# A two-layer attention and MLP kernel: second MLP product from fp16 halves, and small steps moved between VectorE, ScalarE and GpSimd

## The chip, the cores and the metric

The kernel runs as one program on one NeuronCore of a Trainium2 chip. The metric is device time in microseconds (us), from the start of the program to its end, as the median of several executions. One execution was also recorded by the hardware profiler; its rows are quoted below. Five engines work in parallel, each through its own queue in program order: TensorE (PE in the profile; PEld is its weight load), VectorE (DVE), ScalarE (ACT), GpSimd (POOL) and SyncE (SP), which here issues all DMAs. They meet only at semaphores.

## The reference, cut to what matters

The input x is 4 x 2048 x 256 in float32. Two blocks follow one another, each wrapped in layer normalisations and a residual sum:

```
x = x + layernorm(A(layernorm(x)))      # A: full self-attention over each batch of 2048 rows, softmax over axis 1
x = x + layernorm(F(layernorm(x)))      # F: two layers as below
layer(x):
    h = shift_token(x); q, k, v = split(h @ wqkv)         # 8 heads of 64
    q = l2norm(q) * q_scale; k = l2norm(k) * k_scale; q, k = rotary_xpos(q, k)
    o = local_attention(q, k, v)                          # windows of 128 rows, own window and the one before
    x = x + o @ wo
    h = layernorm(shift_token(x)) * ln_g + ln_b
    a, g = split(h @ w1 + b1)                             # 2 x 682 columns
    x = x + (a * gelu(g)) @ w2 + b2                       # w2: 682 x 256, "the second MLP product"
```

## The kernel before, in words

`phase_a` computes A batch by batch and writes the normalised result, the stream of layer one, to DRAM. `phase_b` computes F. It has a prologue, a block of its own in which weights are loaded, scaled and split, and then the main block.

Splitting is how float32 products are made here. A value is split into a high part, rounded to a narrower type, and a low part, the value less its high part; three products (high x high, high x low, low x high: `PARTS`) stand for the full one. In the main block wqkv, wo and the scores go through the fp32r type in this way, and w1 with its input h2T through fp16. The exception is the second MLP product (L955): it multiplies `hid` by `w2`, both plain float32, in 12 products of 128x256 for two windows; the profile has 24 records for them, two for each product.

The main block treats a stream of 128 windows of 128 rows (64 for each layer). All five engines run the same sequence of slots, written out by hand in a function `run(s, r, pairs, layer)`; four slots are unrolled in a loop (`slots`). In slot s TensorE does, in this order: transposes of qr and kr of window s-1 (L847, L854), the q, k and v projections of window s (L869), transposes of the probabilities of window s-2 (L885) and their product with v (L897), scores of window s-1 (L910), the wo product of window s-2 (L923), transposes of the next window's input (L836). The MLP works on pairs of windows: an even slot ends with the first MLP product (L944, 66 records), the odd slot after it with the second (L955). So a pair of slots is one period. The order inside each engine's `run` is fixed, and a wait at any place holds back all that is behind it on that engine.

The other engines in a slot, as far as the change touches them:

- ScalarE: copies of qT and kT, squares of q and k (`sq`, L981 and L983), copy of v (L986), four copies of transposed probabilities (`probsT`, L992), copy of oT (L995), eight exponentials (L1002), in even slots six gelus (L1015).
- VectorE: low parts of qT and kT (L1098, L1100), in even slots the pair's output sum `layer_output` (L1063), statistics of the MLP input h2 (L1107, L1109, L1111), the rotary products of q in three pieces (L1041 to L1043), the normalised MLP input `xh` and its fp16 high part (L1117, L1120), the rotary products of k, in odd slots of layer two the statistics of the final normalisation (`output_stats`), low part of oT (L1090), eight masked score passes (L1138) with `floor_norms` (L1050) inside them, then reciprocals and normalisations of the probabilities in pairs (L1148, L1151), with the residual sum xp (L1162) behind the second pair, in odd slots of layer two `output_norm` (L1084), in even slots six products with the gelu (`hid`, L1174).
- GpSimd: the power that gives 1/std of the MLP input (L1200), six halvings that sum the 64 squares of each head (`halve`, L1190), the low part of xh (L1205), qr (L1209) and the sum of k's rotary terms (L1212), in odd slots of layer two a power for the final normalisation (L1218), the power that gives the 16 inverse norms `rn` (L1223), kr = terms x inverse norms (L1228), the sum xb (L1234), in odd slots of layer two the final residual sum (L1240). kr of window s is what TensorE transposes at L854 near the start of slot s+1.
- SyncE: xp goes to DRAM and comes back, shifted by one row, as h2 (L819, L823, L824); the two fp16 halves of xh are transposed by a DMA into h2T (L813).

## Time and profile before

| | us |
|---|---|
| median of 3 executions | 3123.78 (3122.63 to 3124.51) |
| the profiled execution, its time | 3122.74 |
| its span, first to last instruction | 3120.9 |

The busy shares of the span are PE 95%, PEld 83%, DVE 85%, ACT 60% and POOL 56%. `phase_a` fills the first 650 us, the prologue lasts to about 717 us, and the main block has the rest. A row of the profile's groups gives line, engine, operation, output<-input, count, busy time and mean duration; a row of a timeline gives start, duration and the same names, with the idle time ahead of it in brackets where there was some.

### The profile page before, as it was taken

The page shows a single profiled execution, that of the slowest core. Times are in us where ns is not written, and L with a number is a line of the kernel's source. Part 1 is how long each engine was busy: PE and PEld are TensorE (multiplying, and loading weights), DVE is VectorE, ACT ScalarE, POOL GpSimd, SP SyncE. Part 2 cuts the span into 40 slices and gives each one's busy share as a digit, 9 for nine tenths or more (in the row PEclk, how much of TensorE's full clock was granted, in tenths as well). Part 3 has the DMA queues.
Part 4 walks back from the last instruction along what each step waited for, and adds up shares of the span by engine and source line. Part 5 has one row for each costly group of instructions (what it writes and reads, how often), then busy time and mean ns, then how long its engine had stood idle before and what let it go on. Part 6 is the DMA issues. An engine that isn't in the chain of part 4 may idle for free.

```text
span 3120.9 us, 79791 instructions
## 1 busy us (share of the span) xinstructions
PE 2969.0 (95%) x24952; PEld 2577.5 (83%) x24952; DVE 2654.2 (85%) x7701; ACT 1876.3 (60%) x4322; POOL 1742.8 (56%) x2070
## 2 busy tenths in 40 slices
PE   7999999945999999999999999999999999999997
PEld 4868686844888888888888888888888888888886
DVE  7889898656888888888888888898999999999995
ACT  6252525113666666667666766666666667666763
POOL 0313131125666666666666666676776677767763
PEclk9999999967999999999999999999999999999998
DMA  1212121151111111111111111122221211122121
GB/s 39 62 48 64 46 63 40 54 202 53 47 50 49 56 47 50 52 49 47 50 54 50 49 54 48 51 57 61 61 56 58 59 55 55 58 64 59 56 58 43
DMA packets 273326, 177.65 MB, mean 57 GB/s; under 512 B 95758, under 2 KB 271090, under 8 KB 272754
## 3 DMA queue, kind: packets, MB, share of 16 engines
q1 hardware_dynamic: 273138, 175.50, 19.2%
q8 instruction: 74, 1.21, 0.2%
q14 instruction: 114, 0.93, 0.1%
HBM read 104.08 MB, written 54.54 MB: 51 GB/s over the span
## 4 chain that ended last, share of the span: by engine, by line
PE 73%; POOL 1%; issue 1%; DVE 1%; ACT 0%; DMA 0%; POOLq 0%; SPq 0%; DVEq 0%; ACTq 0%
PE b_ps L869 17%; PE b_ps L944 14%; PE b_ps L955 10%; PE b_ps L897 8%; PE b_ps L885 7%; PE b_ps L923 6%; PE b_ps L910 6%; PE b_ps L854 2%; PE b_ps L847 2%; PE b_ps L836 1%; POOL b_sq L1190 0%; POOL b_rn L1223 0%; DVE b_probs L1138 0%; POOL b_t L1212 0%; DVE b_probs L1151 0%
## 5 line engine op out<-in xcount | busy, mean ns | idle before, releaser
L1002 ACT ACTIVATE b_probs<-b_probs,b_negmax 128x256 f32<-128x256 f32 x1024 | 505.9, 495 | 78.4 <-DVE b_negmax L1138 77.5
L869 PE MATMUL b_ps<-b_wqkv,b_hT_hi 128*128 128x512 f32 x1536 | 492.0, 402 | 1.0 <-DVE b_hT_lo L1026 1.0
L944 PE MATMUL b_ps<-b_h2T,b_w 128*128 128x256 f16 x4224 | 474.4, 274 | 6.4 <-DMA b_h2T<-b_xh_hl 6.4
L944 PEld LDWEIGHTS b_ps<-b_h2T,b_w 128*128 128x128 f16 x4224 | 414.5, 98 | 55.3 <-DMA b_h2T<-b_xh_hl 6.8
L1190 POOL TENSOR_TENSOR b_sq<-b_sq 128x512 f32<-128x512 f32 (+5 forms) x768 | 418.5, 545 | 60.6 <-ACT b_sq L983 20.3
L1223 POOL TENSOR_TENSOR b_rn<-b_ss_min,b_mhalf 128x16 f32<-128x16 f32 x128 | 377.5, 2949 | 109.2 <-DVE b_ss_min L1050 109.0
L1151 DVE TENSOR_SCALAR b_probs<-b_probs,b_rinv 128x256 f32<-128x256 f32 x1024 | 409.6, 442 | 18.2
L1200 POOL TENSOR_TENSOR b_rstd<-b_var,b_mhalf 128x1 f32<-128x1 f32 x128 | 72.0, 562 | 552.9 <-DVE b_var L1111 552.9
L452 PE MATMUL a_ps<-a_xn_hl,a_E 128*128 128x256 f16 x3072 | 344.5, 273 | 8.8 <-DVE a_E L318 8.8
L955 PE MATMUL b_ps<-b_w,b_hid 128*128 128x256 f32 x1536 | 342.2, 379 | 1.2 <-DVE b_hid L1174 1.2
L452 PEld LDWEIGHTS a_ps<-a_xn_hl,a_E 128*128 128x128 f16 x3072 | 299.4, 98 | 44.2 <-ACT a_e L397 9.6
L869 PEld LDWEIGHTS b_ps<-b_wqkv,b_hT_hi 128*128 128x128 f32 x1536 | 282.7, 191 | 54.3 <-ACT b_hT_hi L967 1.4
L1138 DVE CUSTOM_DVE_ANT_0 b_probs<-b_ps,b_mask,b_rn 128x256 f32<-128x256 f32 x768 | 324.5, 478 | 0.0
L955 PEld LDWEIGHTS b_ps<-b_w,b_hid 128*128 128x128 f32 x1536 | 286.8, 190 | 37.9 <-DVE b_hid L1174 1.5
L869 PE MATMUL b_ps<-b_wqkv,b_hT_lo 128*128 128x512 f32 x768 | 302.7, 394 | 0.0
L992 ACT COPY b_probsT<-b_ps 128x512 f32<-128x512 f32 x512 | 264.0, 611 | 4.5 <-PE b_ps L885 4.2
L1015 ACT ACTIVATE b_gl<-b_ps,b_b,b_w_unit 128x256 f32<-128x256 f32 (+1 forms) x384 | 202.8, 561 | 102.8 <-DVE b_hid L1174 70.4
L897 PE MATMUL b_ps<-b_probsT,b_v 128*64 128x128 f32 x4096 | 252.3, 276 | 0.0
L885 PE MATMUL b_ps<-b_ident_f,b_probs 128*128 128x128 f32 x2048 | 245.5, 273 | 3.5 <-DVE b_xpp L1063 2.3
L885 PEld LDWEIGHTS b_ps<-b_ident_f,b_probs 128*128 128x128 f32 x2048 | 232.2, 141 | 20.0 <-DVE b_xpp L1063 2.5
L897 PEld LDWEIGHTS b_ps<-b_probsT,b_v 128*64 128x64 f32 x4096 | 221.4, 137 | 21.6 <-ACT b_probsT L992 18.1
L1174 DVE SCALAR_TENSOR_TENSOR b_hid<-b_ps,b_b1a,b_gl 128x256 f32<-128x256 f32 (+1 forms) x384 | 177.0, 478 | 53.3 <-ACT b_gl L1015 46.9
(139 smaller groups left out, 6218.8 us busy)
## 6 DMA issues: line engine op xcount, KB each, us to landing
b_hx<-xs_dram SPq DMA_DIRECT2D x256, 64.0 KB, 1.9
b_rot<-rot_dram SPq DMA_DIRECT2D x128, 128.0 KB, 2.1
b_xr<-xs_dram SPq DMA_DIRECT2D x128, 128.0 KB, 2.0
xp_dram<-b_xp SPq DMA_DIRECT2D x128, 128.0 KB, 1.8
b_h<-xp_dram SPq DMA_DIRECT2D x256, 64.0 KB, 1.8
a_x_res<-in_L_attn_x_dram SPq DMA_DIRECT2D x64, 128.0 KB, 2.2
x_dram<-a_x SPq DMA_DIRECT2D x64, 128.0 KB, 1.7
xs_dram<-a_xo SPq DMA_DIRECT2D x64, 128.0 KB, 1.8
```

Of the source, the lines that this page charges most:

```text
L452: last = nc.tensor.matmul(ps[:, bank, 0:D], E[:, j, a, i * P:(i + 1) * P], xn_hl[:, b % 2, j, c, :], start=(j == 0 and a == 0 and c == 0), ...
L869: last = nc.tensor.matmul(ps[:, bank, :], hT[:, k, :], wqkv[:, ds(layer(s), 1), part, k, bank * INNER:(bank + 1) * INNER], start=(k == 0 a ...
L885: last = nc.tensor.transpose(ps[:, 3 + p, n * P:(n + 1) * P], probs[:, 2 * p + n // 2, (n % 2) * P:(n % 2 + 1) * P], ident_f[:])
L897: last = nc.tensor.matmul(ps[h * DH:(h + 1) * DH, 7, p * P:(p + 1) * P], v[:, window, (2 * p + h) * DH:(2 * p + h + 1) * DH], probsT[:, p, ...
L944: last = nc.tensor.matmul(ps[:, bank, half * 2 * P:(half + 1) * 2 * P], w1[:, ds(layer(2 * j), 1), wp, k, first:first + P], h2T[:, hp, k, ...
L955: last = nc.tensor.matmul(ps[:, 3, n * D:(n + 1) * D], hid[:, c, n * P:(n + 1) * P], w2[:, ds(layer(2 * j), 1), c, :], start=(c == 0), sto ...
L992: nc.scalar.copy(probsT[:, p, :], ps[:, 3 + p, :]).then_inc(pT_kept, 1)
L1002: nc.scalar.activation(probs[:, h, :], probs[:, h, :], ACT.Exp, bias=negmax[:, h:h + 1], scale=-1.0, accum_out=rowsum[:, h:h + 1]).then_in ...
L1138: nc.vector.tensor_tensor_reduce(probs[:, h, :], head_scores(h), which, rn[:, (r - 1) % 2, h:h + 1], ABOVE_ALL, ALU.add, ALU.min, negmax[: ...
L1151: nc.vector.tensor_scalar(probs[:, h, :], probs[:, h, :], rinv[:, h:h + 1], None, ALU.mult).then_inc(probs_ready, 1)
L1190: nc.gpsimd.tensor_tensor(target, target, sq[:, :, width:2 * width], ALU.add).then_inc(ss_halved, 1)
L1223: nc.gpsimd.tensor_tensor(rn[:, r % 2, :], ss_min[:], mhalf[:], ALU.pow).then_inc(rn_ready, 1)
```

## The change

- The second MLP product: w2 is kept as two fp16 halves, scaled by a power of two, and the pair's output sum multiplies by `w2_unit` to undo the scale (one operation with a product and a sum in place of a plain sum). `hid` is split into two fp16 halves by GpSimd (`hid_halves`: a copy and a subtraction for each of 6 blocks; four blocks at the end of GpSimd's even slot, two early in the odd one). TensorE then does 36 fp16 products of 128x256 in place of the 12 float32 ones, and waits for `hid_lo` in place of `hid_ready`.
- The prologue: w2 and b1 are loaded ahead of the rotary table and wqkv; bounds for the scale of `hid` are found by further reductions on VectorE and a second all-reduce on GpSimd; w1 is scaled in two column parts, each split in its own instruction; w2 is scaled and split; three of the five masks are copied in SBUF instead of loaded.
- The MLP input: `xh` and its fp16 high part are made by ScalarE (`normalise_input`, two activations with scale and bias), in even slots ahead of the probability copies, in odd slots behind them and behind v's copy. The epsilon sum and the bias are made by GpSimd (`var2`, `shift2`). VectorE keeps the statistics, now ahead of `layer_output`.
- The final normalisation: `varf` and `shiftf` on GpSimd, the normalisation itself on ScalarE.
- The sums of squares: one halving on GpSimd, the rest as one reduction on VectorE (`sum_squares`), the floor on GpSimd; the power of 16 columns becomes one of 8 for k, ahead of kr, and one of 8 for q, behind it ("powers behind their sum").
- VectorE: the rotary products of a tensor in two instructions (the second reads the halves in reversed order) in place of three; reciprocals for four heads at a time in place of two.

The main block's part of the diff (semaphore declarations and changed counts left out):

```diff
-                        pe.wait_ge(hid_ready, HC * (j + 1))
+                        pe.wait_ge(hid_lo, HC * (j + 1))
                         if in_range(s - 1):
                             pe.wait_ge(scores_kept, HEADS * (s - 1) + BANK_READ[3])
                         for n in range(2):
                             for c in range(HC):
-                                last = nc.tensor.matmul(ps[:, 3, n * D:(n + 1) * D], hid[:, c, n * P:(n + 1) * P], w2[:, ds(layer(2 * j), 1), c, :],
-                                                        start=(c == 0), stop=(c == HC - 1))
+                                for a, (hp, wp) in enumerate(PARTS):
+                                    last = nc.tensor.matmul(ps[:, 3, n * D:(n + 1) * D], hid_hl[:, hp, c, n * P:(n + 1) * P],
+                                                            w2[:, ds(layer(2 * j), 1), wp, c, :],
+                                                            start=(c == 0 and a == 0), stop=(c == HC - 1 and a == 2))
...
+                def normalise_input(t, r):
+                    if in_range(t):
+                        act.wait_ge(shift2_ready, t + 1)
+                        wait(act, xh_lo, t)
+                        nc.scalar.activation(xh[:], h2[:, (r - 3) % 2, :], ACT.Identity, bias=shift2[:], scale=rstd2[:]).then_inc(xh_ready, 1)
+                        wait(act, h2T_loaded, 16 * t)
+                        nc.scalar.activation(xh_hl[:, 0, :], h2[:, (r - 3) % 2, :], ACT.Identity, bias=shift2[:], scale=rstd2[:]).then_inc(xh_hi, 1)
...
-                        wait(act, ss_ready, s)
+                        wait(act, ss_summed, s)
                         act.wait_ge(q_done, s + 1)
                         nc.scalar.activation(sq[:, 0:HEADS, :], by_head(ps[:, 0, :]), ACT.Square).then_inc(q_sq, 1)
                         act.wait_ge(k_done, s + 1)
                         nc.scalar.activation(sq[:, HEADS:2 * HEADS, :], by_head(ps[:, 1, :]), ACT.Square).then_inc(k_sq, 1)
-                        act.wait_ge(v_done, s + 1)
-                        wait(act, pv_done, s - 2)
-                        nc.scalar.copy(v[:, r, :], ps[:, 2, :]).then_inc(v_kept, 1)
+                    if r % 2 == 0:
+                        normalise_input(s - 3, r)
                     t = s - 2
                     if in_range(t):
                         wait(act, pv_done, t)
                         for p in range(HP):
                             act.wait_ge(pT_done, HP * t + p + 1)
                             nc.scalar.copy(probsT[:, p, :], ps[:, 3 + p, :]).then_inc(pT_kept, 1)
+                    if in_range(s):
+                        act.wait_ge(v_done, s + 1)
+                        wait(act, pv_done, s - 2)
+                        nc.scalar.copy(v[:, r, :], ps[:, 2, :]).then_inc(v_kept, 1)
+                    if r % 2 == 1:
+                        normalise_input(s - 3, r)
...
+                        act.wait_ge(shiftf_ready, f + 1)
+                        wait(act, fin_stored, 16 * f)
+                        for n in range(2):
+                            nc.scalar.activation(fin[:, n, :], xpp[:, n, :], ACT.Identity, bias=shiftf[:, n:n + 1], scale=rstdf[:, n:n + 1]).then_inc(xf_ready, 1)
...
+                        nc.vector.tensor_tensor(by_head(t1[:, n, :]), by_head(ps[:, n, :]), factor(2 * n), ALU.mult).then_inc(terms, 1)
+                                                factor(2 * n + 1).rearrange("p h (c d) -> p h c d", c=2), ALU.mult).then_inc(terms, 1)
...
+                def norm_stats(s, r):
+                    t = s - 3
+                    if in_range(t):
+                        dve.wait_ge(h2_loaded, 32 * (t + 1))
+                        nc.vector.bn_stats(st2[:], h2[:, (r - 3) % 2, :]).then_inc(st2_ready, 1)
+                        wait(dve, shift2_ready, t)
+                        wait_apart(dve, st2_ready, t + 1, passed_dve)
+                        nc.vector.bn_aggr(mv2[:], st2[:]).then_inc(mv2_ready, 1)
...
+                            nc.vector.scalar_tensor_tensor(xpp[:, n, :], ps[:, 3, n * D:(n + 1) * D], w2_unit[:, ds(layer(2 * j), 1)], xb[:, (r - 6 + n) % 4, :],
+                                                           ALU.mult, ALU.add).then_inc(xpp_ready, 1)
...
                     layer_output(pairs - 3, r, layer)
-                    t = s - 3
-                    if in_range(t):
-                        dve.wait_ge(h2_loaded, 32 * (t + 1))
-                        nc.vector.bn_stats(st2[:], h2[:, (r - 3) % 2, :]).then_inc(st2_ready, 1)
-                        wait_apart(dve, st2_ready, t + 1, passed_dve)
-                        nc.vector.bn_aggr(mv2[:], st2[:]).then_inc(mv2_ready, 1)
-                        dve.wait_ge(mv2_ready, t + 1)
-                        nc.vector.tensor_scalar(var2[:], mv2[:, 1:2], EPS, None, ALU.add).then_inc(var2_ready, 1)
                     rotate(s, r, 0, q_sq, q_terms, qr_ready)
-                    t = s - 3
-                    if in_range(t):
-                        dve.wait_ge(rstd2_ready, t + 1)
-                        wait(dve, xh_lo, t)
-                        nc.vector.tensor_scalar(xh[:], h2[:, (r - 3) % 2, :], mv2[:, 0:1], rstd2[:], ALU.subtract, ALU.mult).then_inc(xh_ready, 1)
-                        dve.wait_ge(xh_ready, t + 1)
-                        wait(dve, h2T_loaded, 16 * t)
-                        nc.vector.tensor_copy(xh_hl[:, 0, :], xh[:]).then_inc(xh_hi, 1)
                     rotate(s, r, 1, k_sq, k_terms, kr_ready)
                     output_stats(pairs - 3, r, layer)
+                    sum_squares(s)
                     oT_low(s - 2)
...
+                            if p % 2 == 0:
+                                dve.wait_ge(exp_done, HEADS * t + 2 * p + 4)
+                                nc.vector.reciprocal(rinv[:, 2 * p:2 * p + 4], rowsum[:, 2 * p:2 * p + 4]).then_inc(rinv_ready, 1)
+                                dve.wait_ge(rinv_ready, 2 * t + p // 2 + 1)
...
-                def halve(s, first, end):
-                    if in_range(s):
-                        pool.wait_ge(k_sq, s + 1)
-                        for n in range(first, end):
-                            width = DH >> (n + 1)
-                            target = sq[:, :, 0:width]
-                            wait(pool, ss_halved, HALVINGS * s + n)
-                            nc.gpsimd.tensor_tensor(target, target, sq[:, :, width:2 * width], ALU.add).then_inc(ss_halved, 1)
+                def hid_halves(j, first, end):
+                    if in_range(2 * j):
+                        wait(pool, w2_done, j)
+                        for c in range(first, end):
+                            rows = slice(0, P if c < FULL else REST)
+                            wait_apart(pool, hid_ready, HC * j + c + 1, passed_pool)
+                            nc.gpsimd.tensor_copy(hid_hl[rows, 0, c, :], hid[rows, c, :]).then_inc(hid_hi, 1)
+                            pool.wait_ge(hid_hi, HC * j + c + 1)
+                            nc.gpsimd.tensor_tensor(hid_hl[rows, 1, c, :], hid[rows, c, :], hid_hl[rows, 0, c, :], ALU.subtract).then_inc(hid_lo, 1)
                 def run(s, r, pairs, layer):
                     if r == 0 and in_range(s):
                         nc.gpsimd.tensor_copy(mask_now[:], mask[:, ds((s // SLOTS) % (WPB // SLOTS), 1), :]).then_inc(mask_ready, 1)
                     t = s - 3
                     if in_range(t):
+                        wait_apart(pool, mv2_ready, t + 1, passed_pool)
+                        nc.gpsimd.tensor_scalar(var2[:], mv2[:, 1:2], EPS, None, ALU.add).then_inc(var2_ready, 1)
                         pool.wait_ge(var2_ready, t + 1)
+                        wait(pool, xh_hi, t)
                         nc.gpsimd.tensor_tensor(rstd2[:], var2[:], mhalf[:, 0:1], ALU.pow).then_inc(rstd2_ready, 1)
-                    halve(s, 0, 2)
-                    if in_range(t):
+                        wait_apart(pool, rstd2_ready, t + 1, passed_pool)
+                        nc.gpsimd.tensor_scalar(shift2[:], mv2[:, 0:1], rstd2[:], -1.0, ALU.mult, ALU.mult).then_inc(shift2_ready, 1)
+                    if in_range(s):
+                        pool.wait_ge(k_sq, s + 1)
+                        nc.gpsimd.tensor_tensor(sq[:, :, 0:DH // 2], sq[:, :, 0:DH // 2], sq[:, :, DH // 2:DH], ALU.add).then_inc(ss_halved, 1)
+                    if r % 2 == 1:
+                        hid_halves(pairs - 2, HID_EARLY, HC)
+                    t = s - 3
+                    if in_range(t):
+                        pool.wait_ge(xh_ready, t + 1)
                         pool.wait_ge(xh_hi, t + 1)
                         wait(pool, h2T_loaded, 16 * t)
                         nc.gpsimd.tensor_tensor(xh_hl[:, 1, :], xh[:], xh_hl[:, 0, :], ALU.subtract).then_inc(xh_lo, 1)
                     if in_range(s):
-                        pool.wait_ge(q_terms, 3 * (s + 1))
+                        pool.wait_ge(q_terms, 2 * (s + 1))
                         wait(pool, qT_done, s)
                         nc.gpsimd.tensor_tensor(qr[:], t1[:, 0, :], t2[:, 0, :], ALU.add).then_inc(qr_ready, 1)
-                        halve(s, 2, HALVINGS)
-                        pool.wait_ge(k_terms, 3 * (s + 1))
+                        pool.wait_ge(k_terms, 2 * (s + 1))
                         nc.gpsimd.tensor_tensor(t1[:, 1, :], t1[:, 1, :], t2[:, 1, :], ALU.add).then_inc(kr_sum, 1)
                     j = pairs - 3
                     f = j - NW // 2
                     if r % 2 == 1 and in_range(2 * j) and layer(2 * j) == 1:
+                        wait_apart(pool, mvf_ready, 2 * f + 2, passed_pool)
+                        nc.gpsimd.tensor_scalar(varf[:], mvf[:, :, 1], EPS, None, ALU.add).then_inc(varf_ready, 1)
                         pool.wait_ge(varf_ready, f + 1)
+                        wait(pool, xf_ready, 2 * f)
                         nc.gpsimd.tensor_tensor(rstdf[:], varf[:], mhalf[:, 0:2], ALU.pow).then_inc(rstdf_ready, 1)
+                        wait_apart(pool, rstdf_ready, f + 1, passed_pool)
+                        for n in range(2):
+                            last = nc.gpsimd.tensor_scalar(shiftf[:, n:n + 1], mvf[:, n, 0:1], rstdf[:, n:n + 1], -1.0, ALU.mult, ALU.mult)
+                        last.then_inc(shiftf_ready, 1)
                     if in_range(s):
+                        wait_apart(pool, ss_summed, s + 1, passed_pool)
+                        nc.gpsimd.tensor_scalar(ss_min[:], ss[:], 1e-24, None, ALU.max).then_inc(ss_ready, 1)
                         pool.wait_ge(ss_ready, s + 1)
-                        wait(pool, scores_kept, HEADS * (s - 1))
-                        nc.gpsimd.tensor_tensor(rn[:, r % 2, :], ss_min[:], mhalf[:], ALU.pow).then_inc(rn_ready, 1)
-                    if in_range(s):
-                        pool.wait_ge(rn_ready, s + 1)
+                        nc.gpsimd.tensor_tensor(rn_k[:], ss_min[:, HEADS:2 * HEADS], mhalf[:, 0:HEADS], ALU.pow).then_inc(rnk_ready, 1)
+                        pool.wait_ge(rnk_ready, s + 1)
                         pool.wait_ge(kr_sum, s + 1)
                         wait(pool, kT_done, s)
                         nc.gpsimd.tensor_tensor(by_head(kr[:]), by_head(t1[:, 1, :]),
-                                                rn[:, r % 2, HEADS:2 * HEADS].unsqueeze(2).to_broadcast([P, HEADS, DH]), ALU.mult).then_inc(kr_ready, 1)
+                                                rn_k[:].unsqueeze(2).to_broadcast([P, HEADS, DH]), ALU.mult).then_inc(kr_ready, 1)
+                        wait(pool, scores_kept, HEADS * (s - 1))
+                        nc.gpsimd.tensor_tensor(rn[:, r % 2, :], ss_min[:, 0:HEADS], mhalf[:, 0:HEADS], ALU.pow).then_inc(rn_ready, 1)
                     t = s - 2
                     if in_range(t):
                         pool.wait_ge(xp_ready, t + 1)
                         wait(pool, xpp_ready, t - 3)
                         nc.gpsimd.tensor_tensor(xb[:, (r - 2) % 4, :], xp[:, r % 2, :], b2[:, ds(layer(t), 1), :], ALU.add).then_inc(xb_ready, 1)
+                    if r % 2 == 0:
+                        hid_halves(pairs - 2, 0, HID_EARLY)
```

## Rows read from the trace of the kernel before

**Rows 1.** The page: busy time, share of the span and instructions of each engine.

```profile
PE 2969.0 (95%) x24952; PEld 2577.5 (83%) x24952; DVE 2654.2 (85%) x7701; ACT 1876.3 (60%) x4322; POOL 1742.8 (56%) x2070
```

**Rows 2.** Stretches: busy us of each engine, granted clock, DMA share, GB/s.

```profile
1496.90:1533.50 36.60, 36.60 (x317) 32.68 (x315) 31.64 (x99) 25.19 (x63) 23.67 (x27) 1.00 0.17 50
2630.90:2667.60 36.70, 36.70 (x317) 32.59 (x315) 33.66 (x106) 25.02 (x63) 25.97 (x29) 1.00 0.20 57
```

**Rows 3.** Timeline of PE over one pair of slots.

```profile
1496.75 7.37 PE L944 MATMUL b_ps<-b_h2T,b_w 128*128 128x256 f16 x66
1503.95 0.60 PE L847 MATMUL b_ps<-b_ident_f,b_qr 128*128 128x128 f32 x4
...
1510.80 1.97 PE L897 MATMUL b_ps<-b_probsT,b_v 128*64 128x128 f32 x32
...
1516.05 5.34 PE L955 MATMUL b_ps<-b_w,b_hid 128*128 128x256 f32 x24
1521.23 0.60 PE L847 MATMUL b_ps<-b_ident_f,b_qr 128*128 128x128 f32 x4
1521.67 0.60 PE L854 MATMUL b_ps<-b_ident_f,b_kr 128*128 128x128 f32 x4
```

**Rows 4.** Timeline of POOL, the same pair: kr of the odd slot.

```profile
1519.81 1.04 POOL L1228 TENSOR_TENSOR b_kr<-b_t,b_rn 128x512 f32<-128x512 f32 x1
```

**Rows 5.** Groups of instructions on POOL, by line.

```profile
L1223 POOL TENSOR_TENSOR b_rn<-b_ss_min,b_mhalf 128x16 f32<-128x16 f32 x128 | 377.5, 2949 | 109.2 <-DVE b_ss_min L1050 109.0
...
L1212 POOL TENSOR_TENSOR b_t<-b_t 128x512 f32<-128x512 f32 x128 | 165.5, 1293 | 0.0
...
L1205 POOL TENSOR_TENSOR b_xh_hl<-b_xh,b_xh_hl 128x256 f16<-128x256 f32 x128 | 86.4, 675 | 40.0 <-DVE b_xh_hl L1120 40.0
...
L1200 POOL TENSOR_TENSOR b_rstd<-b_var,b_mhalf 128x1 f32<-128x1 f32 x128 | 72.0, 562 | 552.9 <-DVE b_var L1111 552.9
...
L1218 POOL TENSOR_TENSOR b_rstdf<-b_varf,b_mhalf 128x2 f32<-128x2 f32 x32 | 22.6, 707 | 19.3 <-DVE b_varf L1075 15.8 <-DMA b_x<-x_dram 3.5
...
L1196 POOL COPY b_mask_now<-b_mask 128x256 bf16 (+1 forms) x32 | 13.8, 430 | 0.0
...
L223 POOL TENSOR_TENSOR a_rstd_c<-a_pow_c,a_unscale 128x1 f32<-128x1 f32 x64 | 12.1, 189 | 5.0
...
L210 POOL TENSOR_TENSOR a_rstd_first<-a_var_first,a_mhalf 128x4 f32<-128x4 f32 x4 | 4.8, 1198 | 13.8 <-DVE a_var_first L276 13.8
```

**Rows 6.** Timeline of DVE, ACT and SP in the same pair.

```profile
1504.74 1.06 DVE L1174 SCALAR_TENSOR_TENSOR b_hid<-b_ps,b_b1a,b_gl 128x256 f32<-128x256 f32 x2 [0.26 <-ACT b_gl L1015]
...
1507.71 0.18 DVE L1109 BATCH_NORM_AGGREGATE b_mv<-b_st 128x2 f32<-128x6 f32 x1 [0.15 <-DVE b_st L1107]
...
1502.95 1.02 ACT L1015 ACTIVATE b_gl<-b_ps,b_b,b_w_unit 128x256 f32<-128x256 f32 x2 [1.06 <-DVE b_hid L1174]
...
1507.79 0.60 ACT L983 ACTIVATE b_sq<-b_ps 128x512 f32<-128x512 f32 x1 [0.72 <-PE b_ps L869]
...
1509.64 2.06 ACT L992 COPY b_probsT<-b_ps 128x512 f32<-128x512 f32 x4
1512.81 0.59 ACT L995 CAST b_oT<-b_ps 128x512 fp32r<-128x512 f32 x1 [1.11 <-PE b_ps L897]
...
1521.65 0.38 SPq L824 DMA_DIRECT2D b_h<-xp_dram  x1
```

**Rows 7.** Groups on DVE in the prologue, and its last instruction there (timeline).

```profile
L654 DVE TENSOR_REDUCE p_top<-p_w_f 128x1 f32<-128x2816 f32 x2 | 6.2, 3086 | 0.1
...
715.85 0.36 DVE L681 TENSOR_SCALAR b_b1a<-b_b,p_w_scale 128x6 f32<-128x6 f32 x2
```

**Rows 8.** The page's DMA issues: output<-input, count, size, us from issue to landing.

```profile
b_h<-xp_dram SPq DMA_DIRECT2D x256, 64.0 KB, 1.8
```

**Rows 9.** The chain that ended last, first slots of the main block.

```profile
726.91 1.30 POOL b_sq L1190
...
736.01 1.05 POOL b_kr L1228
```

200 lines of the change are left out of this document (115 added, 85 removed).

## The prediction

> **What bounds the kernel now.** I read first the busy shares and the busy time by stretch. PE is busy 95% of the span [rows 1], and in a period of the main block it is busy all of it: 36.6 of 36.6 us in layer one and 36.7 of 36.7 in layer two, at a granted clock of 1.00 (2.4 GHz), with DVE at 31.6 and 33.7 and POOL at 23.7 and 26.0 [rows 2]. So the period is TensorE's own work, and only less of that work, or a new wait of PE, moves it. Second, PE's timeline, for the length of the slots. I count from the start of the odd slot, 1503.95, as 0: the second MLP product stands at 12.10 to 17.28, then come the next slot's q transposes, and its k transposes at 17.72 [rows 3]. Third, POOL's timeline, for the one result that comes near its need: kr for that even slot is done at 1520.85, which is 16.90, 0.8 ahead of its use [rows 3, 4]. Last the groups by line, for prices.
>
> **The product.** The float32 form takes 5.18 us a pair (1516.05 to 1521.23). The fp16 form is the shape of the first MLP product, which runs 66 records in 7.20 us, 0.109 each [rows 3]; 36 of them are 3.93 us. Gain 1.25 us a pair. Of the 64 pairs two fall in the drain, so 62 x 1.25 = 77.5 us, if nothing new is late. The odd slot becomes 16.03 long, and kr is needed at 16.47.
>
> **GpSimd's odd slot, layer one.** Prices on POOL: a power of 1, 2, 4 and 16 columns took 0.56, 0.71, 1.20 and 2.95 us [rows 5]. One of 8 columns lies between 1.20 and 2.95; on the line through those two it is 1.78, which I take. The small steps (`var2`, `shift2`, floor, `varf`, `shiftf`) have as nearest row a 1-column product at 0.19; their ends are 0.10 and the 0.56 of the power; I take 0.19, plus 0.1 where a wait stands ahead. A float32 to fp16 copy of 256 columns has the mask's copy, 0.43, as nearest row; its ends are 0.2 and the 0.675 of the two-input subtraction into fp16; I take 0.43. The subtraction itself is that 0.675 row [rows 5]. The two-input passes of 512 columns are 1.29 (the first halving 1.30) [rows 5, 9].
> The order is then: mv2 from DVE at 3.94 (DVE's place for it is unmoved) [rows 6]; `var2`, power, `shift2` 1.21, so 5.15; k's squares are done by 4.44 [rows 6], so the halving ends at 6.45; blocks 4 and 5 of `hid`, which DVE ends by about 1.85 [rows 6], cost 1.27 each (copy, subtraction, 0.17 of waits): 9.0. The high part of xh comes from ACT: probability copies from about 5.5 to 7.5, v 0.5, two activations that I price as the pair of gelus, 1.02 [rows 6]: 9.0 as well. Low part 0.75: 9.75. qr and k's sum 2.5: 12.25. Floor 0.3, power 1.85, kr 1.1: 15.5. That is 1.0 ahead of 16.47, about the room there was. The four blocks of the even slot's end don't reach in: the first block of `hid` is there at about -1.15, four cost 5.0 at most, 3.9 is just ahead of mv2. Layer one keeps its full gain: of the 62 steady pairs 33 run before the final normalisation's steps begin, 33 x 1.25 = 41.
>
> **Layer two.** Here the odd slot also holds `varf`, its power, and two `shiftf`: 0.29 + 0.78 + 0.48 = 1.55, ahead of kr. So kr comes at 17.05, 0.6 late, where before `varf` was DVE's and the powers stood in room. Behind it wait q's power 1.78, xb 0.7 to 0.8 and the final sum 1.29; GpSimd is then at about 20.9, 4.9 into the even slot, plus 0.46 for the mask in every other one. `var2` to `shift2` takes 1.21 more, and now ACT stands at `normalise_input` ahead of the probability copies: shift2 at 6.1 or 6.55, activations to 7.1 or 7.6, first copy 0.5 later, 7.6 or 8.1. PE wants it for its product with v at 6.85 [rows 3] plus the 0.6 that it is already late: another 0.15 or 0.65, on average 0.4. Together 1.0 lost of 1.25, so 29 x 0.25 = 7 gained.
> The Trainium skill (GPSIMD Engine Reference, Engine selection) advises against GpSimd for elementwise work, two-input operations being about twice VectorE's time and one-input ones roughly line rate. The rows agree on the first (675 and 1293 ns for 256 and 512 columns); by the second a copy would be an estimated 0.1 shorter than mine, kr 0.2 earlier, and the sum 6 lower.
>
> **What is taken from other engines** costs nothing in a period, since PE hides it. DVE loses xh and its cast, the third rotary piece, half of the reciprocals, and gains one reduction of 512 columns, about 0.6 by 1.1 ns a column [rows 7], between k's rotation and oT's low part, where it waited anyhow. The h2 load ends 1.8 after its issue at 1521.65 [rows 6, 8], 19.5, which in a shorter odd slot is 3.5 into the even one: mv2 comes 0.8 later there than before, at about 4.2, shift2 at 5.4, ACT's activations end at 6.4 and the first copy at 6.9, against 6.85. That costs 0.05 at most in layer one; without the move ahead of `layer_output` it would cost 0.7. In the odd slot ACT ends its activations at 9.0 and took oT up at 8.86 before [rows 6]: 0.15 late, and the wo product has about as much room. I take zero for it, with 0.2 a slot as the other end.
>
> **The start of the main block.** The first four slots are a chain through GpSimd: from k's squares at 726.9 to kr at 737.1, 10.2 us [rows 9]. New: halving 1.3, qr and sum 2.55, floor 0.3, power 1.85, kr 1.1: 7.1. That is 3 us in each of four slots, 12; between 6 (where PE and the scores take over as the bound) and 15.
>
> **The prologue** ends with DVE, at 716.2 [rows 7]. DVE must now finish w2's maxima before the scale is known (3072 columns at 1.1 ns, 3.4 [rows 7]), run some 12 more small steps (2), and split w2 (3.3): 9 in all. The ends are 2 (the shorter mask copy, less contention) and 20 (wqkv lands behind 1.4 MB more). The sum takes 9.
>
> **The drain.** The last two blocks of `hid` are halved behind the last gelu, 1.7 to 2 us; the final normalisation's small steps add 0.6 twice; the product is 1.25 shorter: +2, between -1 and +6.
>
> **Sum,** against the profiled execution's own 3122.7 (the span is 1.8 less, and the median of the runs 1.0 more, which I leave): 3122.7 + 9 - 12 - 41 - 7 + 2 = 3074.
>
> **Rivals.**
> - GpSimd keeps up in layer two as well: its small steps overlap, or copies are at their lower end. For it: kr is only 0.6 late by my count, within the error of seven estimated steps. Against it: POOL would be busy over 90% of a layer-two period. 3122.7 + 9 - 12 - 77.5 + 2 = 3044.
> - ScalarE's new order delays oT in the odd slot or the copies in the even one, by 0.2 each, in all pairs: 62 x 0.4 = 25 less gain, 3098. For it: 0.0 to 0.15 of room. Against: DVE is earlier now.
> - The other side: GpSimd's chain from mv2 to kr is late in layer one and far too late in layer two. With every unknown half way to its upper end (copy 0.55, power 2.37, small steps 0.375) the chain is 1.4 longer in layer one: kr 0.45 late, gain 33 x 0.8 = 26. In layer two it is 2.0 longer, kr at 19.0, 2.55 late, and with rn, xb and the final sum behind it the even slot's first copy 1.0 late: 3.55 - 1.25 = 2.3 lost in 29 pairs, 67. 3122.7 - 1 - 26 + 67 = 3163, slower. It decides from about 1.7 us more a pair than I have counted for layer two.
> - ACT needs another table for Identity: a load of 1.28 ahead of each use, 2.6 a pair in ACT's two tight places, 62 x 1.35 = 84 more, 3206. The trace before has copies and squares beside Exp and Gelu without loads of their own, no row has Identity. The Trainium skill (ScalarE: Activation LUTs, Table sets: the hidden batching unit) names identity among the fillers in every set, which speaks against this.
> - The change doesn't do what it says: three fp16 products take as long as the float32 one, by weight loads. Against it, the 66 records beside it [rows 3]. 3122, within 0.2%.
>
> **Chances.** Forecast 0.45 (its own range 3055 to 3095); full gain 0.30; ScalarE's order 0.10; GpSimd late in both 0.08; tables 0.03; no shorter product 0.04. A measurement of this kernel tells 0.2%, 6 us, from no change. Faster 0.86 (the first three, and a little), same 0.05, slower 0.09. The range leaves out the slow cases and the edge of the full gain: 3035 to 3115.
>
> **What would show it.** The second product at 3.9 us a pair. A layer-one period of 35.3 with PE without a gap; a layer-two period of about 36.3 with two waits of PE, k transposes on kr (0.6) and the product with v on `probsT` (0.4), and POOL at over 32 us busy. Ramp slots 3 us shorter, prologue 9 longer. It is wrong if layer one shows a wait of PE above 0.3 a pair, if layer two shows none or over 2 us, or if the power of 8 columns is over 2.3 us.

## The result, and the profile after

The changed kernel takes 3157.46 us (median of 4 runs, 3153.39 to 3158.82) against 3123.2 for the kernel before, timed beside it: ratio 1.0108, interval 1.009 to 1.0125. It is slower by 34 us; the forecast was 3074. The profiled execution has a span of 3157.0, 36.1 longer than before.

The page of the changed kernel, busy time by engine, against [rows 1]:

```profile
PE 2926.8 (93%) x25720; PEld 2507.4 (79%) x25720; DVE 2415.2 (77%) x6734; ACT 2036.9 (65%) x4644; POOL 2065.3 (65%) x2807
```

PE is busy 42 us less and the kernel is 36 longer, so PE is idle 78 us more. In PE's groups by line the second product alone fell by 77 us (342.2 to 264.9, L955 and L1007); the rest of PE's busy time rose by 35, 10 of it in the projections and 9 in the product with v. Two stretches, one period of layer one and one of layer two, with the columns of [rows 2]:

```profile
1521.70:1558.10 36.40, 35.99 (x329) 31.53 (x328) 28.37 (x85) 27.09 (x66) 28.18 (x38) 1.00 0.18 51
2672.10:2709.60 37.50, 35.94 (x329) 31.57 (x328) 29.01 (x89) 28.21 (x69) 30.89 (x42) 1.00 0.20 56
```

Before, PE was busy for the whole of either period. Now 0.4 and 1.6 are idle, at the full granted clock. From the starts of the 64 first MLP products the span divides like this (us, against the kernel before):

| stretch | forecast | measured |
|---|---|---|
| up to the first MLP product (802.1 to 805.0) | -3 | +2.9 |
| its pairs 0 to 32, period 36.56 to 36.46 | -41 | -3 |
| pairs 32 to 62, period 36.57 to 37.66 from pair 34 on | -7 | +31 |
| from pair 62's to the end (51.7 to 56.7) | +2 | +5 |

The next table tells where in a slot it stands. It has the mean start of each of TensorE's products, counted from the slot's first q transpose, over 20 pairs of layer one (L1) and 24 of layer two (L2), read from the timelines of PE. I use it for every kernel below. Columns: k transposes (kr), projections (qkv), transposes of probabilities (pT), product with v (pv), wo, MLP product (w1 or w2), end of the slot.

```
kernel    slot     kr    qkv   pT    pv    wo     mlp    end
before    even L1  0.44  0.79  4.99  6.83  10.34  12.09  19.29
before    odd  L1  0.44  0.79  4.99  6.83  10.34  12.08  17.27
changed   even L1  0.44  0.79  5.35  7.47  11.13  12.87  20.08
changed   even L2  2.03  2.44  6.71  8.78  12.44  14.18  21.39
changed   odd  both 0.44 0.79  5.07  6.91  10.62  12.36  16.29
a3        even L1  0.43  0.79  5.07  6.91  10.48  12.40  19.61
a4        even L2  0.61  1.20  5.52  7.56  11.22  12.96  20.16
b1        even L1  0.44  1.46  5.91  8.04  11.70  13.44  20.65
b1        even L2  0.44  1.21  5.53  7.51  11.17  12.91  20.12
d1        even L1  0.44  0.79  5.07  6.91  10.49  12.41  19.62
d1        even L2  0.61  1.20  5.49  7.33  10.91  12.84  20.05
d4        even L1  0.44  1.38  5.68  7.51  11.01  12.75  19.96
d4        odd  L2  0.43  0.79  5.07  6.91  12.44  14.19  18.18
```

The second product did become 1.25 shorter: the odd slot's last part is 3.93 (16.29 - 12.36), as worked out from [rows 3]. The even slot gave it back, 0.8 in layer one and 2.1 in layer two.

**Layer two.** The timeline of PE and POOL in the changed kernel, the end of an odd slot that began at 2655.82:

```profile
2672.11 0.60 PE L898 MATMUL b_ps<-b_ident_f,b_qr 128*128 128x128 f32 x4
2674.14 0.66 PE L905 MATMUL b_ps<-b_ident_f,b_kr 128*128 128x128 f32 x4 [1.43 <-POOL b_kr L1301]
...
2663.48 0.67 POOL L1245 TENSOR_TENSOR b_hid_hl<-b_hid,b_hid_hl 42x256 f16<-42x256 f32 x1
2665.41 0.68 POOL L1272 TENSOR_TENSOR b_xh_hl<-b_xh,b_xh_hl 128x256 f16<-128x256 f32 x1 [1.26 <-ACT b_xh_hl L1029]
2666.05 1.27 POOL L1276 TENSOR_TENSOR b_qr<-b_t 128x512 f32<-128x512 f32 x1
2667.28 1.28 POOL L1278 TENSOR_TENSOR b_t<-b_t 128x512 f32<-128x512 f32 x1
2668.64 0.23 POOL L1284 TENSOR_SCALAR b_varf<-b_mvf 128x2 f32<-128x2 f32 x1
2668.95 0.73 POOL L1287 TENSOR_TENSOR b_rstdf<-b_varf,b_mhalf 128x2 f32<-128x2 f32 x1
2669.90 0.59 POOL L1290 TENSOR_SCALAR b_shiftf<-b_mvf,b_rstdf 128x1 f32<-128x1 f32 x2 [0.22 <-POOL b_rstdf L1287]
2670.57 0.39 POOL L1295 TENSOR_SCALAR b_ss_min<-b_ss 128x16 f32<-128x16 f32 x1
2671.05 1.83 POOL L1297 TENSOR_TENSOR b_rn_k<-b_ss_min,b_mhalf 128x8 f32<-128x8 f32 x1
2672.97 1.04 POOL L1301 TENSOR_TENSOR b_kr<-b_t,b_rn_k 128x512 f32<-128x512 f32 x1
```

Read GpSimd's rows as one queue. It is full from `xh_lo` (L1272) to kr (L1301) and ends 18.2 after the slot's start, where 16.5 was wanted; ahead of `xh_lo` it stands idle for 1.26 and waits for ScalarE. The changed kernel's waits of PE, columns: waiting line, releaser, total us, times, longest:

```profile
PE b_ps L905 <- POOL b_kr L1301: 48.8, 31, 3.8
```

**Layer one.** The even slot that begins at 1558.08, timelines of four engines:

```profile
1561.64 0.43 DVE L1130 BATCH_NORM_STATS2 b_st<-b_h 128x6 f32<-128x256 f32 x1 [0.94 <-DMA b_h<-xp_dram]
1562.20 0.18 DVE L1133 BATCH_NORM_AGGREGATE b_mv<-b_st 128x2 f32<-128x6 f32 x1
1562.51 0.88 DVE L1146 SCALAR_TENSOR_TENSOR b_xpp<-b_ps,b_w_unit,b_xb 128x256 f32<-128x256 f32 x2
...
1563.68 0.27 POOL L1260 TENSOR_SCALAR b_shift<-b_mv,b_rstd 128x1 f32<-128x1 f32 x1 [0.21 <-POOL b_rstd L1258]
...
1563.98 0.60 ACT L1027 ACTIVATE b_xh<-b_h,b_shift,b_rstd 128x256 f32<-128x256 f32 x1 [1.44 <-POOL b_shift L1260]
1564.49 0.59 ACT L1029 ACTIVATE b_xh_hl<-b_h,b_shift,b_rstd 128x256 f16<-128x256 f32 x1
1564.98 2.02 ACT L1053 COPY b_probsT<-b_ps 128x512 f32<-128x512 f32 x4
...
1563.52 1.96 PE L936 MATMUL b_ps<-b_ident_f,b_probs 128*128 128x128 f32 x16 [0.21 <-DVE b_xpp L1146]
1565.60 2.12 PE L948 MATMUL b_ps<-b_probsT,b_v 128*64 128x128 f32 x32
```

Two waits follow from the same DMA. VectorE's output sum stands behind the statistics, which wait 0.94 for h2; the transposes of the probabilities need the PSUM bank that this sum reads, so they start at 5.44. And ScalarE's copies stand behind `xh`, which waits 1.44 for shift2, so the product with v starts at 7.5.

### The profile page after: what moved, and what is told of

It is laid out like the page before. It is cut to its first block and busy times, and to the rows that moved or that the text cites. A ratio compares the mean times of both kernels' runs of the same rounds, so it can differ in the third digit from the quotient of the medians.

```text
span 3157.0 us, 81578 instructions
## 1 busy us (share of the span) xinstructions
PE 2926.8 (93%) x25720; PEld 2507.4 (79%) x25720; DVE 2415.2 (77%) x6734; ACT 2036.9 (65%) x4644; POOL 2065.3 (65%) x2807
## 5 line engine op out<-in xcount | busy, mean ns | idle before, releaser
L920 PE MATMUL b_ps<-b_wqkv,b_hT_hi 128*128 128x512 f32 x1536 | 498.9, 406 | 1.9 <-DVE b_hT_lo L1102 1.0
L1206 DVE TENSOR_SCALAR b_probs<-b_probs,b_rinv 128x256 f32<-128x256 f32 x1024 | 345.7, 389 | 9.0
L1163 DVE TENSOR_TENSOR b_oT<-b_ps,b_oT 128x512 fp32r<-128x512 f32 x128 | 88.5, 692 | 326.0 <-ACT b_oT L1064 326.0
L1194 DVE CUSTOM_DVE_ANT_0 b_probs<-b_ps,b_mask,b_rn 128x256 f32<-128x256 f32 x768 | 317.7, 479 | 0.0
L1245 POOL TENSOR_TENSOR b_hid_hl<-b_hid,b_hid_hl 128x256 f16<-128x256 f32 (+1 forms) x384 | 258.4, 673 | 30.8
L948 PE MATMUL b_ps<-b_probsT,b_v 128*64 128x128 f32 x4096 | 260.8, 280 | 12.0 <-ACT b_probsT L1053 10.2
L1007 PE MATMUL b_ps<-b_w,b_hid_hl 128*128 128x256 f16 x2304 | 264.9, 274 | 3.0 <-POOL b_hid_hl L1245 3.0
L1007 PEld LDWEIGHTS b_ps<-b_w,b_hid_hl 128*128 128x128 f16 x2304 | 226.5, 98 | 30.2 <-POOL b_hid_hl L1245 3.2
L1243 POOL CAST b_hid_hl<-b_hid 128x256 f16<-128x256 f32 (+1 forms) x384 | 152.3, 397 | 123.7 <-DVE b_hid L1228 102.5
L1297 POOL TENSOR_TENSOR b_rn_k<-b_ss_min,b_mhalf 128x8 f32<-128x8 f32 x128 | 219.0, 1711 | 10.7
```

The lines of the kernel that those rows point to most:

```text
L920: last = nc.tensor.matmul(ps[:, bank, :], hT[:, k, :], wqkv[:, ds(layer(s), 1), part, k, bank * INNER:(bank + 1) * INNER], start=(k == 0 a ...
L948: last = nc.tensor.matmul(ps[h * DH:(h + 1) * DH, 7, p * P:(p + 1) * P], v[:, window, (2 * p + h) * DH:(2 * p + h + 1) * DH], probsT[:, p, ...
L1007: last = nc.tensor.matmul(ps[:, 3, n * D:(n + 1) * D], hid_hl[:, hp, c, n * P:(n + 1) * P], w2[:, ds(layer(2 * j), 1), wp, c, :], start=(c ...
L1194: nc.vector.tensor_tensor_reduce(probs[:, h, :], head_scores(h), which, rn[:, (r - 1) % 2, h:h + 1], ABOVE_ALL, ALU.add, ALU.min, negmax[: ...
L1206: nc.vector.tensor_scalar(probs[:, h, :], probs[:, h, :], rinv[:, h:h + 1], None, ALU.mult).then_inc(probs_ready, 1)
L1245: nc.gpsimd.tensor_tensor(hid_hl[rows, 1, c, :], hid[rows, c, :], hid_hl[rows, 0, c, :], ALU.subtract).then_inc(hid_lo, 1)
```

## The experiments

Theory of waits: the new orders hold TensorE in four places (kr in layer two, the output sum, the probability copies, oT), and the product is as good as forecast. The rival put the loss in slower instructions, contention or the clock. Each kernel is timed beside the kernel before. Line numbers are each kernel's own.

**a1, a2, a3: the orders of the even slot.**

```diff
 # a1, VectorE                                 # a2, ScalarE; a3 = a1 + a2
+layer_output(pairs - 3, r, layer)             -if r % 2 == 0: normalise_input(s - 3, r)
 norm_stats(s, r)                               (four copies to probsT)
-layer_output(pairs - 3, r, layer)             +if r % 2 == 0: normalise_input(s - 3, r)
```

> On VectorE layer_output stands ahead of norm_stats again, as before the change; all else is the changed kernel. Theory of waits: in even slots the output sum no longer waits for h2's load, so TensorE's transposes of the probabilities start at about 5.0 us in the even slot in place of 5.4. But ScalarE's probability copies stay behind normalise_input, which waits for shift2, and mv2 now comes 0.7 later; so the product with v does not come earlier and may come up to 0.7 later: 3157 to 3185 us, no gain. Rival (the lost gain is not in the order of waits but in slower instructions, contention or the clock): the same time as the changed kernel, 3157, and no move of the product with v.

> On ScalarE the two activations of normalise_input in even slots stand behind the four probability copies; all else is the changed kernel. Theory of waits: the product with v no longer waits for shift2, only for the transposes, which are late by the output sum: it comes at about 7.3 in place of 7.5 in the even slot. Gain 0.2 to 0.3 us a pair in both layers, 12 to 18 us, less what the later high part of xh costs GpSimd in layer two: 3140 to 3155 us. Rival (slower instructions): no change, 3157.

> Both edits together: the output sum ahead of the statistics on VectorE, and normalise_input behind the probability copies on ScalarE, in even slots. Theory of waits: the two waits cover one another, so that the pair gives far more than the sum of the two alone: transposes at 5.0, product with v at 6.8 in the even slot, layer-one period 35.6 to 35.7 in place of 36.4, so 0.7 to 0.8 in 33 pairs, and half of that in layer two, where GpSimd is late: 3157 - 25 - 10 = 3122 us, 3115 to 3135. Rival (slower instructions or clock): under 10 us of gain, 3147 or more.

Measured: a1 3158.99, a2 3151.98, a3 3141.12 us (a3's ratio to before 1.0063, 1.0046 to 1.0079); a1 and a2 are as expected, a3 gained half of what was expected (3122). Alone, a1 brings nothing (pT at 5.07, pv still at 7.50) and a2 5.5 us (pv at 7.28); together 16. A wait behind another is worth nothing until the first is gone. The even slot of a3 in layer one, began at 1550.78, timelines of PE and ACT:

```profile
1555.85 1.91 PE L936 MATMUL b_ps<-b_ident_f,b_probs 128*128 128x128 f32 x16
1557.68 1.97 PE L948 MATMUL b_ps<-b_probsT,b_v 128*64 128x128 f32 x32
...
1556.48 2.05 ACT L1051 COPY b_probsT<-b_ps 128x512 f32<-128x512 f32 x4 [1.24 <-PE b_ps L936]
1558.39 0.63 ACT L1027 ACTIVATE b_xh<-b_h,b_shift,b_rstd 128x256 f32<-128x256 f32 x1
```

Neither wait is left. But the gain is 0.47 a pair in layer one, not 0.75: `xh` is now later, the first MLP product starts 0.39 behind the transposes ahead of it in place of 0.22, and wo is 0.07 late. In layer two it is 0.14 (37.66 to 37.52), since the late kr had covered one of the two waits.

**a4: the final normalisation put back** (epsilon sum and normalisation on VectorE, its power on GpSimd, no `shiftf`).

> The final normalisation is as before the change: the epsilon sum and the normalisation on VectorE, only its power on GpSimd, and nothing of it on ScalarE. Else the changed kernel. Theory of waits: GpSimd's odd slot in layer two is shorter by the epsilon sum, the two shifts and their waits, about 1.2 us, so kr is done at 17.0 in place of 18.2, TensorE's wait for it falls from 1.6 to about 0.5 a pair, 29 pairs: 3157 - 32 = 3125 us, 3115 to 3135; layer one unchanged. Rival (kr is late by GpSimd's instructions running slower beside VectorE's, which now has more of them): 3150 or more.

Measured: 3122.49 (ratio 0.9999, 0.999 to 1.0009). The wait for kr, same view as above:

```profile
PE b_ps L905 <- POOL b_kr L1299: 7.5, 2, 3.9
```

Only the two waits of the main block's start are left; a rest of 0.17 a pair shows in the table, without a record. Layer two goes from 37.66 to 36.52, layer one stays. The theory held: three small steps and two waits on a full queue cost 35 us. The edit also takes two activations from ScalarE, and no run parts the two; but the wait that went is the one for kr.

**b1, b2: the hole in GpSimd's queue filled.**

```diff
 # b1, GpSimd, odd slots only; b2 = b1 + a4
-xh_hl[:, 1] = xh - xh_hl[:, 0]     (waits for xh_hi)
 qr = ...
 t1[:, 1] = t1[:, 1] + t2[:, 1]
+xh_hl[:, 1] = xh - xh_hl[:, 0]
```

> In odd slots GpSimd makes the low part of xh behind the sum of k's terms, so that it no longer stands waiting for ScalarE's high part (1.3 us idle before it) ahead of qr, the sum and kr; all else is the changed kernel. Theory of waits: kr of the odd slot comes 1.3 to 1.9 earlier, at 16.3 to 16.9, and TensorE's wait for it in layer two (1.6 a pair) goes or is under 0.4; layer two's period becomes about layer one's, 36.4 to 36.6 in place of 37.66, so 29 x 1.15 = 33: 3124 us, 3118 to 3132. Layer one is unchanged, since kr is not late there. The h2T transfer starts later in the odd slot, with the whole odd slot as room. Rival (GpSimd has too much work in layer two, whatever its order): kr's lateness only moves to the even slot's shift2 and copies, 3145 or more.

> The final normalisation as before the change (ScalarE and GpSimd freed of it) and the low part of xh behind the sum of k's terms in odd slots. With the final normalisation put back alone, TensorE's wait for kr was down to 0.17 a pair in layer two, and the time 3122.5. Theory of waits: both edits act on the same wait, so together they give only that rest and a little: layer two's period equals layer one's, 36.4, 3119 us, 3114 to 3123. Rival (each shortens GpSimd's load and the load is what counts): the gains add, 3090.

Measured: b1 3140.6, b2 3161.68. In layer two b1 does what was expected, 36.46. But layer one, which should have stayed, goes from 36.46 to 37.00, with a wait for the low part of hT (qkv at 1.46). b2, which the theory put at 3119, is 39 us above a4. So here the theory of waits fell short. The end of the odd slot, first in the changed kernel, timelines of DVE and POOL (the next slot starts at 1521.72), then in b1, timelines of DVE, POOL and PE (1530.63):

```profile
1519.36 1.14 DVE L1206 TENSOR_SCALAR b_probs<-b_probs,b_rinv 128x256 f32<-128x256 f32 x4
...
1518.63 1.67 POOL L1297 TENSOR_TENSOR b_rn_k<-b_ss_min,b_mhalf 128x8 f32<-128x8 f32 x1
1520.38 1.04 POOL L1301 TENSOR_TENSOR b_kr<-b_t,b_rn_k 128x512 f32<-128x512 f32 x1
```

```profile
1528.26 1.70 DVE L1206 TENSOR_SCALAR b_probs<-b_probs,b_rinv 128x256 f32<-128x256 f32 x4
...
1527.97 1.04 POOL L1307 TENSOR_TENSOR b_kr<-b_t,b_rn_k 128x512 f32<-128x512 f32 x1
...
1532.08 0.72 PE L920 MATMUL b_ps<-b_wqkv,b_hT_hi 128*128 128x512 f32 x2 [0.41 <-DVE b_hT_lo L1102]
```

Four normalisations take 1.14 beside GpSimd's power and 1.70 beside kr's multiplication. It is not that each runs slower. The view of line L1206 in this stretch gives the four durations (minimum, median, maximum):

```profile
L1206 DVE TENSOR_SCALAR b_probs<-b_probs,b_rinv x4: 340/341/910, 1528.3 to 1529.6; 128x256 f32<-128x256 f32 x4
```

One of the four takes 0.91, the others their usual 0.34: the first stands until kr is done at 1529.02, and ends at 1529.17. Everything behind it is later: the residual sum and the DMA of h2 it feeds (issued at 1.61 in b1's even slots, at 1.05 in the changed kernel's), and hT's low part. In b2 the same holds in layer two as well: the load of h2 is issued at 1.82 there, at 1.05 in a4, and TensorE waits for the output sum behind it (23.4 us in 36 waits; 6.6 in 9 in a4).

**e1: kr moved away from them again** (b1, q's power ahead of kr in place of behind it).

> As b1 (low part of xh behind the sum of k's terms in odd slots), but with q's power ahead of kr instead of behind it. In b1 layer one became 0.55 slower a pair: TensorE waits 0.7 for the low part of hT, since VectorE's four first normalisations of the probabilities took 1.70 us in place of 1.14 (0.43 in place of 0.29 each) while GpSimd computed kr, a multiplication of 512 columns, beside them, and the two after them 1.10 in place of 0.88 beside q's power and xb; beside a power alone they take 0.29. Theory of contention (two-input passes of GpSimd slow VectorE's SBUF-to-SBUF passes, powers don't): kr now lies 1.7 later, the first four take about 1.14 again, TensorE's wait for hT_lo falls to 0.3 or less, layer one's period from 37.0 back to 36.4 or 36.6; in layer two kr is 1.3 late again, 37.6: 3140.6 - 15 + 33 = 3158. Rival (VectorE is late in b1 by its own order or by ScalarE): layer one stays at 37.0, 3173.

Measured: 3149.27; layer one 36.50, layer two 37.22. Timelines of DVE and POOL in e1 (next slot at 1526.85):

```profile
1524.47 1.14 DVE L1206 TENSOR_SCALAR b_probs<-b_probs,b_rinv 128x256 f32<-128x256 f32 x4
...
1526.06 1.65 DVE L1206 TENSOR_SCALAR b_probs<-b_probs,b_rinv 128x256 f32<-128x256 f32 x2
...
1525.78 1.04 POOL L1309 TENSOR_TENSOR b_kr<-b_t,b_rn_k 128x512 f32<-128x512 f32 x1
```

The slow stretch follows kr: the first four are at 1.14 again, and the two that now lie beside kr and xb take 1.65 together. That is the contention, shown by moving its cause. My reading of what it costs was half wrong: the wait for hT's low part didn't shrink (qkv at 1.60), since the delay only moved behind the residual sum. What came back is the residual sum, so the load of h2 and the copies (pv 1.85 behind pT in place of 2.13).

**b3, b4, d3: what the product is worth in three orders.** b3 is the changed kernel with the float32 product, b4 the kernel before with the fp16 product and its prologue.

> The changed kernel with the second MLP product as one float32 product again (w2 scaled, hid not split, GpSimd free of the 12 instructions for its halves). TensorE's odd slot is 1.25 longer. Theory of waits: that length is also room, so the even slot's waits for the output sum, for shift2 and for kr go, and only the odd slot's wait for oT stays: period 36.9 in both layers, against 36.4 and 37.7 of the changed kernel, so +15 in layer one, -22 in layer two, -4 in the prologue: 3146 us, 3138 to 3156. So the fp16 product would be worth about nothing in this schedule. Rival (the product's gain is intact and the loss stands elsewhere): 3157 + 77 = 3234. Second rival (the halves of hid cause every wait, the moves none): 3125 or less.

> The kernel before with the fp16 second product alone: the changed prologue, and on GpSimd the halves of hid (four blocks at the end of its even slot, two behind the first two halvings of the odd one); six halvings, one power of 16 columns, VectorE's small steps and the order of ScalarE as before. Theory of waits: GpSimd's odd slot gets 2.5 us more, of which 1.1 go into the idle time ahead of the 16-column power; kr comes at 16.9 + 1.4 = 18.3 where 16.5 is needed, 1.85 late against 1.25 gained, and 0.5 to 0.6 more in layer two with its extra power: 3123 + 12 (prologue) + 2 + 33 x 0.6 + 29 x 1.15 = 3190 us, 3175 to 3205. So the product needs the moves; they aren't wrong as such. Rival (the moves cost the gain and the product alone is free): 3123 + 14 - 77 = 3060.

Measured: b3 3167.57 (3146 expected), b4 3226.83 (3190 expected). In the changed kernel the product is worth 10 us: 0.48 a pair in layer one (36.94 to 36.46), nothing in layer two (37.63 to 37.66). b3's layer two was expected at 36.9; kr is still 0.3 late and the copies 0.6, without any halves of `hid`. So in layer two the waits stand there with either product. b4 shows the other side: on the old order the halves of `hid` make kr late (1.2 a pair in layer one, 0.7 in layer two), and more than expected in layer two, 39.1 a pair. The moves were needed for the product. Part of b4's excess is this, the group of one VectorE instruction on 2 columns, in the groups by line of the kernel before, a4, b4 and d4 (mean ns last):

```profile
L1075 DVE TENSOR_SCALAR b_varf<-b_mvf 128x2 f32<-128x2 f32 x32 | 7.0, 217 | 1.1
```

```profile
L1152 DVE TENSOR_SCALAR b_varf<-b_mvf 128x2 f32<-128x2 f32 x32 | 12.0, 374 | 1.1
```

```profile
L1126 DVE TENSOR_SCALAR b_varf<-b_mvf 128x2 f32<-128x2 f32 x32 | 50.1, 1564 | 1.1
```

```profile
L1148 DVE TENSOR_SCALAR b_varf<-b_mvf 128x2 f32<-128x2 f32 x32 | 75.8, 2367 | 1.1
```

**d1: a3 and a4 together, and three variants of it.** f1 also puts odd slots' `normalise_input` behind the cast of oT and `xh_lo` between qr and k's sum; d3 has the float32 product; d4 has `xh` and its fp16 part on VectorE as before, without `shift2`.

> Three of the moves taken back together: the output sum ahead of the statistics on VectorE, ScalarE's normalise_input behind the probability copies in even slots, and the whole final normalisation as before the change. Product, halvings, reduction and split powers stay. Theory of waits: layer one as with the first two edits alone, period 35.95; layer two has the same even slot plus 0.17 of wait for kr, 36.1; 3157 - 0.5 x 33 - 1.55 x 29 = 3096 us, 3090 to 3104, faster than both kernels. Rival (the edits only shift the wait to another engine in layer two): 3110 or more.

> As d1, and in odd slots ScalarE's normalise_input stands behind the cast of oT, with GpSimd making the low part of xh between qr and the sum of k's terms, so that kr keeps its time. Theory of waits: the wo product of the odd slot starts 1.6 behind the scores in place of 1.8, 0.2 a pair in both layers, 12 us less than d1: 3084. Rival (the odd slot's 0.2 is VectorE's low part of oT, late for another reason): no change against d1.

> As d1, with one float32 product for the second MLP layer (hid not split). Theory of waits: with the three moves taken back nothing but TensorE's own work and the small waits bind, so the product costs its 1.25 less 0.3 to 0.4 that the longer odd slot gives back (h2T and hT_lo no longer late, kr no longer late in layer two): period 36.9 in both layers, 3105 + 33 x 0.9 + 29 x 0.55 - 3 = 3148; then the fp16 product is worth about 40 us here, where it was worth 10 in the changed kernel. Rival (the product's gain is whole): 3105 + 77 = 3182. Second rival (it gives nothing in any order): 3105.

> As d1, with the MLP input's normalisation and its fp16 high part on VectorE again, between the rotary products of q and k, and without shift2; ScalarE has nothing of the moves left. Theory of waits with contention: wo of the odd slot starts 0.2 earlier and the first MLP product 0.17 earlier, kr of the odd slot is 1.2 earlier and so in time in layer two, but now lies beside VectorE's first normalisations of the probabilities, so that hT_lo comes late as in b1 (0.4 to 0.7 a pair): about the time of d1, 3098 to 3112. Rival (no contention, ScalarE's order is the only cost): 3105 - 62 x 0.37 = 3082 or less. Second rival (VectorE's 0.6 more a slot makes it the bound): 3130 or more.

Measured: d1 3105.41 (ratio 0.9945, 0.9928 to 0.9961), f1 3134.03 (3084 expected), d3 3162.55 (3148 expected), d4 3144.94 (3098 to 3112 expected). d1 is faster than both kernels, by 52 us than the changed one and 17 than the one before. It misses its own expectation by 9: in layer two the projections wait 0.24 a pair for hT's low part and kr is 0.17 late.

d3 less d1 is 57: the product is worth 57 of 77 us once the waits are gone. d3's period is 37.15 where 36.9 was expected; the even slot keeps its waits (19.61).

f1 gained the 0.2 at wo in odd slots (10.41), but a pair of layer one is 0.7 longer than d1's. The timeline of DVE in f1:

```profile
1527.39 0.18 DVE L1207 RECIPROCAL b_rinv<-b_rowsum 128x4 f32<-128x4 f32 x1 [0.58 <-ACT b_probs L1071]
1527.61 1.93 DVE L1210 TENSOR_SCALAR b_probs<-b_probs,b_rinv 128x256 f32<-128x256 f32 x4
```

ScalarE's exponentials were behind the moved step, so the reciprocals wait, and the normalisations slide under kr (1.93). TensorE's q transposes then wait for the residual sum (18.8 us in 35 waits; 5.9 in 2 in d1).

In d4 layer one came as the contention has it (36.01, with qkv at 1.38 against d1's 0.79, made good by the rest of the pair). In layer two wo of the odd slot waits 2.0 for oT's low part (59.0 us in 30 waits), and that stands behind `varf` on VectorE, which takes 2.37 us in the mean for 2 columns (above). One of them, timelines of DVE and POOL in d4:

```profile
2577.23 2.60 DVE L1148 TENSOR_SCALAR b_varf<-b_mvf 128x2 f32<-128x2 f32 x1
...
2576.65 0.67 POOL L1279 TENSOR_TENSOR b_xh_hl<-b_xh,b_xh_hl 128x256 f16<-128x256 f32 x1
2577.28 1.29 POOL L1283 TENSOR_TENSOR b_qr<-b_t 128x512 f32<-128x512 f32 x1
2578.52 1.29 POOL L1285 TENSOR_TENSOR b_t<-b_t 128x512 f32<-128x512 f32 x1
```

It starts while GpSimd subtracts, two sums follow without a gap, and it ends 0.03 behind the second. In a4 the same instruction starts beside a subtraction too, one for `hid_lo` that ends 0.36 later, and takes 0.37. The changed kernel's epsilon sum on GpSimd can't meet this collision, at a price on GpSimd's queue; in a4 and d1 only the times keep the two apart. The second rival of d4, VectorE as the bound by its 0.6 more a slot, is not what TensorE waits for: VectorE is busy 35.4 of 37.7 in such a pair, but 2.4 of that are this one hold.

**g1, h1, h2, h3, h4: the 0.08 of the projections.** In every kernel with the changed constants the projections take 4.28 us a slot, 4.20 before, without a wait. Groups by line of the kernel before, the changed one and h4:

```profile
L869 PE MATMUL b_ps<-b_wqkv,b_hT_hi 128*128 128x512 f32 x1536 | 492.0, 402 | 1.0 <-DVE b_hT_lo L1026 1.0
```

```profile
L920 PE MATMUL b_ps<-b_wqkv,b_hT_hi 128*128 128x512 f32 x1536 | 498.9, 406 | 1.9 <-DVE b_hT_lo L1102 1.0 <-issue 0.9
```

```profile
L871 PE MATMUL b_ps<-b_wqkv,b_hT_hi 128*128 128x512 f32 x1536 | 500.1, 407 | 1.0 <-DVE b_hT_lo L1028 1.0
```

```diff
 # h1: kernel before            # h4: kernel before             # g1, h3: d1
 w2 = sb("w2", ...)             +sb("pad_a", [P, 8])            w2_unit = sb("w2_unit", ...)
+sb("pad", [P, 2])               hT_hi, hT_lo = sb(...)         +sb("pad", [P, 14])    # g1
                                +sb("pad_b", [P, 8])            +sb("pad", [P, 8])     # h3
```

> As d1, with 56 bytes of padding per partition behind the 8 bytes of w2_unit, so that all tiles behind it (hT_hi, hT_lo, oT, mask and so on) lie at the same distance from a 64-byte line as in the kernel before. In the changed kernel the stretch of the q, k and v projections takes 4.28 us a slot where it took 4.20 before, with no wait and the same instructions; every kernel with the changed constants shows it, whatever its product or order. Theory of placement: the stretch is 4.20 again, 126 x 0.08 = 10 us less than d1. Rival (the 0.08 comes from something else, such as other traffic in SBUF): 4.28 stays, same time as d1.

> The kernel before with nothing but 8 unused bytes per partition behind w2, where the changed kernel has w2_unit: all tiles behind it lie 8 bytes further on. Theory of placement: the projections of q, k and v take 4.28 us a slot in place of 4.20, 126 x 0.08 = 10 us more: 3133. Rival (the 0.08 is no matter of addresses): 4.20, 3123.

> As d1, with w2_unit's 8 bytes taken from the unused end of mhalf, so that b2, wo, the masks, hx, hT_hi, hT_lo, v, kT and the rest up to the squares have their addresses of the kernel before. Theory of placement: the projections take 4.20 us a slot again, 3105 - 10 = 3095. Rival (no matter of addresses): 4.28, 3105.

> As d1, with 32 bytes of padding per partition behind w2_unit. Small tiles are rounded up to 32 bytes each, so that w2_unit had moved all behind it by 32, and the 56 bytes of g1 by 96; both leave hT_hi and hT_lo (the stationary operands of the projections) 32 past a multiple of 64 bytes, where the kernel before has them on a multiple. Here they lie on one. Theory of alignment: the projections take 4.20 us a slot, 3105.4 - 10 = 3095. Rival (another tile's place, or the total of shifts): 4.28, 3105.

> The kernel before with 32 bytes of padding ahead of hT_hi and 32 behind hT_lo: only these two tiles lie 32 past a multiple of 64 bytes, all before them is unmoved and all behind them is moved by 64. Theory of alignment: the projections take 4.28 us a slot as in h1, 3133. Rival (it is not these tiles): 4.20, 3123.

Measured: h1 3133.95 (ratio 1.0034, 1.0021 to 1.0046), h4 3134.35 (1.0034, 1.0022 to 1.0046), both with 4.28; g1 3108.88, h2 3105.95, h3 3105.83, all at 4.28 to 4.30; none of these three gave the 10 us back. So placement is shown: unused bytes, and in h4 only around two tiles, cost the kernel before 11 us, 0.15 a pair of it in the projections. The rule is not. The distances rest on a count of the declared tiles, each rounded up to 32 bytes; no trace shows an address. By this count h1 shifts hT by 32, and so does h2, whose edit was to leave hT where the kernel before has it: `mhalf` and `w2_unit` take one unit of 32 more than `mhalf` did. h3 puts hT on a multiple of 64 and is as slow as 32 past one. Only the kernel before's own layout showed 4.20 in these runs, and it stays open which tile's place matters.

## Why the prediction was wrong

The product's 3.93 us and nearly all prices on GpSimd came out as worked out: a cast copy 0.40 (0.43 taken), the power of 8 columns 1.71 and 1.69 (1.78), the small steps 0.23 to 0.30 (0.19 and waits of 0.1). Four steps failed.

1. "Layer one keeps its full gain": 3 us of 41. The prediction's own sign, a wait above 0.3 a pair in layer one, is there: 0.4 idle, and 0.8 in the even slot's length. The gain needed the even slot to follow. I had counted the chain from h2's load to the end of ScalarE's first copy to 6.9 and "0.05 at most"; the product with v starts at 7.5. h2 and the statistics came as forecast (4.3, not 4.2); `var2` to `shift2` took 1.57, not 1.21, as each small step and its wait is a tenth or so longer. And I had not asked at all what the output sum holds once it stands behind a DMA: the transposes' bank. a3 shows the pair of them at 16 us, 17 on top of a4.
2. "kr comes at 17.05" in layer two: 18.19. Named in the right place, sized at a third: 0.5 because `xh_lo` waited longer for ScalarE (10.27, not 9.75, behind copies, v and two activations), 0.4 in the three steps of the final normalisation (1.93, not 1.55), the rest in floor and power. With nothing to absorb it, each tenth was a tenth of TensorE, 29 times. a4: 35 us.
3. "ScalarE's order... I take zero": oT 0.2 a slot late in odd slots, 12 us, the other end that I had given.
4. Not in the sum at all: placement (10 us, h1 and h4), which nothing in the trace of before could show, and contention between VectorE and GpSimd. Contention costs the changed kernel's normalisations less than it cost before (389 ns in the mean, 442 before); it is why filling the hole (b1, b2) or moving work back (d4) failed.

d1, with the waits of steps 1 and 2 taken back, is still 31 us above the forecast: some 22 of them are in layer one, whose period is 36.00 where 35.31 was forecast, by steps 3 and 4 and by 0.24 in the even slot (wo 0.07 and the first MLP product 0.17 late).

The prologue was 10 longer at the main block's start and the first four slots 7 shorter, not 9 and 12. The drain was 5, not 2. Most of that is the last product, 7.00 against 3.93 for the same 36 records: PE had stood idle for 2.95 ahead of it, and the granted clock over it was 0.57, most of it at the lower level, 1.2 GHz. The kernel before had 1.22 idle there, and its last product ran in 5.45 at a granted clock of 1.00. Timeline of PE in the changed kernel:

```profile
3128.20 9.87 PE L995 MATMUL b_ps<-b_h2T,b_w 128*128 128x256 f16 x66 [8.38 <-DMA b_h2T<-b_xh_hl]
3141.02 7.00 PE L1007 MATMUL b_ps<-b_w,b_hid_hl 128*128 128x256 f16 x36 [2.95 <-POOL b_hid_hl L1245]
```

Of the rivals the slower one came within 6 us (3163), with its chance at 0.08, but in part by luck: it had kr late in layer one, where kr was on time and the copies were late. Tables and a product without gain are out: ScalarE's activations ran at 0.60 and 0.59 us. The error of method was one: places with "0.0 to 0.15 of room" were costed at nothing or at 0.05, and each of them is met again in all 62 periods.

## What to carry to other kernels

When the bound engine gets shorter by 1.25 in a period, every other engine's room shrinks by 1.25 too: list each result with its time of need in the shorter period, and treat room under the sum of the small errors as a wait. A step put ahead of another on an in-order queue costs what the step waits for, not what it takes; ask it first of those that wait for a DMA. And before moving small steps from one engine to the other to save their time, look what two-input passes of GpSimd lie beside VectorE's SBUF passes at the new times.

## What the runs showed of the hardware

A GpSimd pass with two inputs holds up VectorE's passes between SBUF tiles; a power on GpSimd does not. The clearest rows are in the prologue of the changed kernel, timelines of DVE and POOL:

```profile
681.58 7.78 DVE L672 TENSOR_TENSOR p_top_sq<-p_top 128x1 f32<-128x1 f32 x1
...
704.54 10.23 DVE L715 SCALAR_TENSOR_TENSOR b_w<-p_w_f,p_w1a_scale,b_w 128x1408 f16<-128x1408 f32 x1
714.70 1.67 DVE L715 SCALAR_TENSOR_TENSOR b_w<-p_w_f,p_w_scale,b_w 128x1408 f16<-128x1408 f32 x1
...
680.53 8.81 POOL L629 TENSOR_TENSOR p_rot_all<-p_rot_all,p_head_scale 128x4096 f32<-128x4096 f32 x1 [29.81 <-DMA p_head_scale<-in_L_ffn_k_scale_dram]
...
703.17 10.13 POOL L629 TENSOR_TENSOR p_rot_all<-p_rot_all,p_head_scale 128x4096 f32<-128x4096 f32 x1 [7.30 <-issue]
```

A product of one column takes 7.78 us and ends with GpSimd's, at 689.3; a pass that takes 1.67 alone takes 10.23, to 1.5 behind GpSimd's end at 713.3. In the main block the trace of the kernel before gives the form of it, over its 1024 normalisations: the 254 that start while kr or xb runs all end 0.15 behind the end of that pass, and of the 762 that start beside the power none takes over 0.36. So one VectorE instruction is held to the end of GpSimd's, and the next run at their usual pace. The Trainium skill (SBUF — State Buffer, Who interferes with whom) has the two share a pair of ports as a lock that the first to issue keeps for its whole instruction. The rows above and `varf` beside a subtraction and two sums (2.60) agree. The powers do not fit: they have two inputs in SBUF and take 1.67 to 2.95 us, and the normalisations beside them are not held.

The second is placement: the same matmuls, 18 a slot, are 2% slower (4.28 against 4.20 us) after unused bytes moved some tiles, 11 us in the kernel before (h1, h4), cause open.
